# Moving the maxima's transposes, the gates' matmuls and ScalarE's layer norms inside one round of the attention

## The chip, the core and the metric

The program runs on one core of a Trainium2 chip. The metric is the device time of one execution in microseconds (us). The engines are TensorE (PE in the views; PEld is its weight load), VectorE (DVE), ScalarE (ACT), GpSimd (POOL) and SyncE (SP), which here only issues DMAs. Each runs its own list of instructions in order, and they meet at semaphores.

## What is computed

A decoder block on `x` of 16 sequences of 256 tokens of width 256. The change touches the first of its three parts, and the layer norm and gates of the second:

```python
x = x + attn(layernorm(x), W_qkv, W_out)                  # causal, 16 heads of 16
x = x + xattn(layernorm(x), ctx, ctx, ifgate_w, ifgate_b, outnorm_w)
x = x + ffn(layernorm(x), router_w, router_b, up, down)   # 8 experts, top 2

# in attn
attn = softmax(q @ k.T * scale + causal_mask)
out = (attn @ v).reshape(B, -1, S); y = einsum('bds,nhd->bsd', out, W_out)
# in xattn, an mLSTM in its parallel form: gates from concat(q, k, v) @ ifgate_w.T + ifgate_b
```

## The kernel before, in words

The kernel has three stages, one after the other: the attention with the preparation of the second part (`attn_steps`, to about 365 us), the mLSTM (`mlstm_steps`), and the experts. The change is in the first alone.

`attn_steps` yields the steps of 22 rounds `i` from -2 to 21. All five engines walk the same list in the same order, and each does its own part of a step. So a step that is moved in the list moves on every engine that has work in it, and on no other. In a full round, for sequence `b = i`:

- `S1` (two, P = 0 and 1) and `S0`: bf16 scores (L505 a mask, L513 the products), from which VectorE takes row maxima (L897, L902) into `mxn`. `Mp` splits the maxima into two bf16 parts (L910, L912), TensorE transposes them (L639), and ScalarE copies them to `MT` (L1227).
- `T0` (two) and `T2`: transposed scores in f32 (L532) with the maxima added (L537), for sequence `i-1`. ScalarE takes exponentials (L1179 behind `T0`, L1185 behind `T2`), two of 128x1024 for each step, GpSimd zeroes above the diagonal (L1338). `PV`: attention times values for `i-2` (L554), copied to `OTs` (L1191). `A4`: transposes of it for `i-2` (L599), scaled by VectorE (L921 to L925) and sent through DRAM by DMA.
- `QK` and `VX`: projections of sequences `i+1` and `i` (L568, L581); the second half of `VX` transposes what came back for `i-3` (L590), which VectorE adds to `x` (L916).
- Layer norms: `A0s` and `A6s` are the statistics (VectorE L840 to L845, GpSimd L1311 and L1314). `A0n` and `A6n` are ScalarE's two instructions that apply them: `xn` for `i+2`, and `QN` for `i-4` (both L1158). `AX` has TensorE transpose `QN` and then `xn` (L614). ScalarE and VectorE split each into two bf16 parts (L1218 and L933 for `QN`, L1223 and L938 for `xn`). `A6c` does the same with the context (L1210, L1350).
- `MG` is the last step of a round: the gates of sequence `i-5` (L630, 24 matmuls of 16 columns; VectorE adds the bias to `Gq`, L943), then the transposes of the maxima of `i`, in the same pair of banks.

PSUM is used as four pairs of banks. The steps that need one (a user) take them in turn, and user n waits until user n-4 has been read:

```python
def pair_of(*user):
    return pairs[place[user] % 4]
def pair_free(w, *user):
    i = place[user]
    ...
    kind, b, *u = users[i - 4]
```

So a user that is added or moved also changes who waits for whom. A full round has 19 users before and after the change. In the rounds that have no gates yet (`i` below 5), it has 19 before and 18 after. Before, the end of a round is, in order, `VX`, `A6n`, `T2`, `Mp` (VectorE's part), `A4`, `AX`, `MG`, and the next round begins with `S1`, `T0`, `PV`.

Of the kernel before, what the change touches and what calls it, by code (L numbers as in the profile page):

```python
# [71 lines left out]
def attn_steps():  # L72


    for i in range(-2, B + 6):
        if ok(i):
            yield "load", 2 * i, 0
            yield "load", 2 * i + 1, 0
            yield "S1", i, 0
        if ok(i - 1):  # L80
            yield "T0", i - 1, 0
        if ok(i - 2):
            yield "PV", i - 2, 0
        if ok(i + 2):
            yield "A0s", i + 2, 0
        if ok(i):
            yield "S1", i, 1
            yield "split", 2 * i, 0
        if ok(i + 1):
            yield "QK", i + 1, 0  # L90
        if ok(i - 4):
            yield "A6s", i - 4, 0
        if ok(i + 2):
            yield "A0n", i + 2, 0
        if i == -2:
            yield "weights", 0, 0
        if ok(i - 1):
            yield "T0", i - 1, 1
        if ok(i):
            yield "S0", i, 0  # L100
            yield "split", 2 * i + 1, 0
        if i > B and ok(i - 2):
            yield "A4", i - 2, 0
        if ok(i) or ok(i - 3):
            yield "VX", i, 0
        if ok(i - 4):
            yield "A6n", i - 4, 0
        if ok(i - 1):
            yield "T2", i - 1, 0
        if ok(i):  # L110
            yield "Mp", i, 0
        if ok(i - 4):
            yield "A6c", i - 4, 0
        if i <= B and ok(i - 2):
            yield "A4", i - 2, 0
        if ok(i + 2) or ok(i - 4):
            yield "AX", i, 0
        if ok(i) or ok(i - 5):
            yield "MG", i, 0
# [59 lines left out]
def build(nc, x, ctx_in, ctx_t, wqkv, wout, wg, bg, gain, wr, br, wup, wdn, cst, out):  # L179
# [6 lines left out]
    with st:  # L186
# [176 lines left out]
        for kind, b, P in steps:  # L363
            if kind in ("S1", "T0"):
                users += [(kind, b, P, u) for u in range(2)]
            elif kind in ("S0", "T2"):
                users += [(kind, b, u) for u in range(2)]
            elif kind in ("QK", "VX", "PV", "A4", "AX", "MG") or (kind, b) == ("weights", 2):
                users.append((kind, b))
# [5 lines left out]
        def pair_free(w, *user):  # L375
# [21 lines left out]
            elif kind == "A4":  # L397
                w.wait_ge(on_.sem, on_.at(b))
            elif kind == "AX":
                w.wait_ge(xl_.sem, xl_.at(b + 2))  # L400
                w.wait_ge(qnl.sem, qnl.at(b - 4))
            elif kind == "MG":
                w.wait_ge(mt_.sem, mt_.at(b))
                w.wait_ge(ga_.sem, ga_.at(b - 5))
# [80 lines left out]
        def tensor_attn(e, w):  # L485
            for kind, b, P in steps:
# [129 lines left out]
                elif kind == "MG":  # L616
                    pair_free(w, "MG", b)
                    ps = pair_of("MG", b)
                    if ok(b - 5):
                        m = b - 5  # L620
                        v = spl(m)
                        w.wait_ge(cl_.sem, cl_.at(m))
                        w.wait_ge(qnl.sem, qnl.at(m))
                        w.wait_ge(wgs, 1)
                        for tt in range(2):
                            n = 0
                            for sx in range(2):
                                for dk in range(2):
                                    for hx, hw in ((0, 0), (0, 1), (1, 0)):
                                        t = e.matmul(ps[:, 1, 16 * tt:16 * tt + 16], v[:, sx, hx, dk, 128 * tt:128 * tt + 128],  # L630
                                                     WGs[:, dk, hw, 16 * sx:16 * sx + 16], start=n == 0, stop=n == 11, skip_group_check=True)
                                        n += 1
                        t.then_inc(gate.sem, 1)
                    if ok(b):
                        bb = ps[:, 0, :].bitcast(BF)
                        w.wait_ge(mp_.sem, mp_.at(b))
                        for a in range(2):
                            for tt in range(2):
                                t = e.transpose(bb[:, 256 * a + 128 * tt:256 * a + 128 * tt + 128],  # L639
                                                Mp[:, tt, a, :, :].rearrange("p n c -> p (n c)"), idb[:, :])  # L640
                        t.then_inc(mpT.sem, 1)
# [242 lines left out]
        def vector_attn(e, w):  # L884
            for kind, b, P in steps:
# [19 lines left out]
                elif kind == "Mp":  # L905
# [255 lines left out]
        def scalar_attn(e, w):  # L1161
            for kind, b, P in steps:
# [481 lines left out]
```

## Time and profile before

| what | us |
|---|---|
| median of 3 runs (1127.26 to 1127.62) | 1127.43 |
| the profiled execution, its time | 1128.98 |
| its span in the trace | 1127.2 |
| busy: PE 885.7, DVE 691.3, POOL 576.1, ACT 473.0 | |

In the timelines a row is a run of like instructions: start, duration from the first start to the last end, engine, line and operation, tiles written and read, and in brackets how long the engine had been idle and what released it. Neighbours on one engine overlap by some 0.1 us, since an instruction's end is counted until its results have landed; so the distance between two starts is what a step takes of its engine.

### The profile page before, as it was taken

What the parts mean: (1) busy time and instruction counts of PE and PEld (TensorE: products, weight loads), DVE (VectorE), ACT (ScalarE), POOL (GpSimd) and SP (SyncE); (2) the same over time, 40 slices, a digit from 0 to 9 for tenths busy, and PEclk for the clock granted to TensorE, in tenths of its full rate; (3) what the DMA queues carried; (4) which work ended last, traced back from release to release, by engine and by line L of the source; (5) the groups of instructions that cost most, each with busy time, mean ns of one, the idle gap of its engine ahead of it and who ended that gap; (6) DMA issues with size and microseconds to landing.
All of it is one profiled execution on the core that took longest, in us unless ns stands there. A gap on an engine that the chain in (4) does not pass through costs nothing.

```text
span 1127.2 us, 31616 instructions
## 1 busy us (share of the span) xinstructions
PE 885.7 (79%) x11680; PEld 670.1 (59%) x11768; DVE 691.3 (61%) x1524; ACT 473.0 (42%) x842; POOL 576.1 (51%) x784
## 2 busy tenths in 40 slices
PE   5888999998982187677666640699999999999995
PEld 3566666665652065455444520578787787787874
DVE  4767776766652667787877873355555555555553
ACT  2656666665652153443443421233333333333331
POOL 2455565646552455677777775134434434344433
PEclk8999999998986598988999965799999999999998
DMA  8113334342335232333333323233333333333322
GB/s 260 39 40 70 110 77 123 74 123 69 90 96 149 78 114 69 114 112 104 115 118 108 103 88 113 72 49 50 49 50 49 50 49 50 49 49 51 48 40 24
DMA packets 130350, 92.48 MB, mean 82 GB/s; under 512 B 74176, under 2 KB 111168, under 8 KB 130080
## 3 DMA queue, kind: packets, MB, share of 16 engines
q1 hardware_dynamic: 116784, 72.10, 23.4%
q0 software_dynamic: 13296, 17.83, 9.5%
q8 instruction: 104, 1.70, 0.6%
q10 hardware_dynamic: 128, 0.53, 0.2%
q14 instruction: 38, 0.31, 0.1%
HBM read 54.38 MB, written 37.12 MB: 81 GB/s over the span
## 4 chain that ended last, share of the span: by engine, by line
PE 52%; DVE 13%; POOL 11%; ACT 9%; DMA 6%; issue 6%; SPq 1%; POOLq 1%; DVEq 0%; ACTq 0%
PE pair L807 17%; PE pair L820 9%; PE pair L822 7%; POOL sm L1387 4%; PE pair L568 4%; PE pair L554 3%; PE pair L532 3%; DVE SD L1006 2%; DMA o_scr<-On 2%; POOL SD L1379 2%; PE pair L581 2%; DMA STG<-wup_in 2%; POOL xs_scr L1395 1%; PE pair L778 1%; DVE hh L1040 1%
## 5 line engine op out<-in xcount | busy, mean ns | idle before, releaser
L807 PE MATMUL pair<-XTs,WU 128*128 128x128 bf16 x3408 | 285.4, 220 | 5.2 <-issue 2.7
L807 PEld LDWEIGHTS pair<-XTs,WU 128*128 x3408 | 239.2, 98 | 72.9 <-issue 8.6
L1420 POOL DMA_INDIRECT out_d<-XB x71 | 114.0, 1606 | 241.1 <-DVE XB L1150 223.2
L820 PE MATMUL pair<-WD,Hh 128*128 x480 | 181.5, 379 | 0.0
L1294 ACT ACTIVATE Hf<-pair 128x512 f32<-128x512 f32 x142 | 84.8, 597 | 224.4 <-PE pair L807 224.4
L1141 DVE CAST Hh<-Hf 128x512 bf16<-128x512 f32 x142 | 62.9, 443 | 177.1 <-ACT Hf L1294 177.1
L822 PE MATMUL pair<-WD,Hl 128*128 x568 | 154.9, 273 | 4.7
L1338 POOL TENSOR_SCALAR_AFFINE_SELECT PT<-PT 128x512 f32<-128x512 f32 (+1 forms) x96 | 74.4, 788 | 71.3 <-ACT PT L1179 62.8
L707 PE MATMUL pair<-QB,QC 128*128 128x256 bf16 (+1 forms) x768 | 87.2, 253 | 22.0 <-DVE SD L1006 21.2
L1143 DVE TENSOR_TENSOR Hl<-Hf,Hh 128x512 bf16<-128x512 f32 x142 | 99.8, 703 | 4.9
L1249 ACT ACTIVATE SD<-pair 128x512 f32<-128x512 f32 (+1 forms) x128 | 60.9, 492 | 98.4 <-PE pair L699 96.1
L1379 POOL TENSOR_SCALAR_AFFINE_SELECT SD<-SD 128x256 f32<-128x256 f32 x128 | 57.7, 457 | 76.5 <-DVE SD L1006 75.7
L897 DVE TENSOR_REDUCE mxn<-pair 128x4 f32<-128x1024 f32 x64 | 75.2, 1217 | 27.8 <-PE pair L513 27.7
L1006 DVE TENSOR_TENSOR SD<-pair,SD 128x512 f32<-128x512 f32 (+1 forms) x128 | 70.6, 553 | 28.9 <-ACT SD L1249 19.1
L707 PEld LDWEIGHTS pair<-QB,QC 128*128 128x128 bf16 x768 | 61.3, 100 | 36.4 <-DVE SD L1006 21.7
L1179 ACT ACTIVATE PT<-pair 128x1024 f32<-128x1024 f32 x64 | 62.0, 1025 | 37.0 <-PE pair L537 37.0
L1395 POOL DMA_INDIRECT xs_scr<-XB,WGf x64 | 68.2, 1066 | 18.1 <-issue 16.5
L532 PE MATMUL pair<-Q,K 32*128 32x128 f32 (+1 forms) x1024 | 66.4, 360 | 13.1 <-DVE Gq L943 7.7
L1408 POOL TENSOR_SCALAR ix<-XB,TE 128x1 f32<-128x1 f32 x71 | 64.8, 912 | 17.9 <-DMA XB<-xs_scr 17.9
L532 PEld LDWEIGHTS pair<-Q,K 32*128 32x128 f32 x1024 | 42.3, 189 | 26.6 <-ACT MT L1227 14.3
L902 DVE TENSOR_REDUCE mxn<-pair 128x8 f32<-128x1024 f32 x32 | 37.7, 1220 | 33.0 <-PE pair L513 33.0
L699 PE MATMUL pair<-WD 128*128 128x256 bf16 (+1 forms) x256 | 43.9, 254 | 17.7 <-DMA WD<-g_scr 11.5
(217 smaller groups left out, 1824.5 us busy)
## 6 DMA issues: line engine op xcount, KB each, us to landing
XB<-xs_scr SPq DMA_DIRECT2D x71, 130.0 KB, 2.1
STG<-wup_in SPq DMA_DIRECT2D x32, 256.0 KB, 4.4
q_scr<-SPL SPq DMA_DIRECT2D x16, 512.0 KB, 4.0
STG<-wdn_in SPq DMA_DIRECT2D x32, 256.0 KB, 2.8
o_scr<-On SPq DMA_DIRECT2D x32, 128.0 KB, 4.1
Mm<-o_scr SPq DMA_DIRECT2D x16, 256.0 KB, 2.9
CnT<-ctxt_in SPq DMA_DIRECT2D x16, 256.0 KB, 4.1
QC<-q_scr SPq DMA_DIRECT2D x16, 256.0 KB, 3.3
```

Of the source, the lines that this page charges most:

```text
L532: e.matmul(o, K[rows, r, par, a, k0:k0 + 128], Q[rows, r, a, 256 - wd:256], start=True, stop=False, skip_group_check=True)
L707: t = e.matmul(sbk[:, wd * dk:wd * dk + wd], v[:, hc, dk, s0:s0 + 128], q[:, hq, dk, t0:256], start=n == 0, stop=n == 2)
L807: t = e.matmul(upb[r][k][:, 128 * (fm % 4):128 * (fm % 4) + 128], WU[:, bass.ds(reg[j] * 4096 + off, 128)], XTs[:, r, hx, dk, :], start=n ...
L820: e.matmul(yb[r][:, 0:512], Hh[:, r, hsl], WD[:, bass.ds(reg[i] * 4096 + 512 * fk, 512)], start=fk == 0, stop=False, skip_group_check=True)
L822: t = e.matmul(yb[r][:, 0:256], Hl[:, r, hsl], WD[:, bass.ds(reg[i] * 4096 + 512 * fk, 256)], start=False, stop=fk == 7, skip_group_check= ...
L897: e.tensor_reduce(mxn[:, 1, P, 2 * u:2 * u + 2, :], pair_of("S1", b, P, u)[:, :, :].rearrange("p j (r c) -> p j r c", r=2), AX.X, ALU.max, ...
L1006: e.tensor_tensor(SD[:, un % 6, 0:2 * wd], sbb[un % 2][:, 0:2 * wd], SD[:, un % 6, 0:2 * wd], ALU.mult).then_inc(sd_.sem, 1)
L1143: e.tensor_tensor(Hl[:, r, hs], Hf[:, r, hs], Hh[:, r, hs], ALU.subtract).then_inc(hlo.sem, 1)
L1294: e.activation(Hf[:, r, hs], upb[r][k][:, :], ACT.Gelu).then_inc(gel.sem, 1)
L1379: e.affine_select(out=dg, in_=dg, pattern=[[0, 2], [1, 128]], compare_op=ALU.is_ge, fill=0.0, base=0, channel_multiplier=-1).then_inc(sz_. ...
L1395: e.indirect_dma_start(out=xs, out_offset=bass.IndirectOffsetOnAxis(ap=SLI[:, m % 2, k, tt:tt + 1], axis=0), in_=XB[:, 4 * m + tt, :], in_ ...
L1420: e.indirect_dma_start(out=out, out_offset=bass.IndirectOffsetOnAxis(ap=XS[:, i % NX, 256:257].bitcast(I32), axis=0), in_=Yf[:, i % NY, :] ...
```

## The change

`MG` is split into two users. `Mp` now has all of the maxima: VectorE's split of them has become a step of its own, `Mq`, directly behind `S0`. TensorE's transposes stand directly behind `T2`, in a pair of their own, and ScalarE's copy to `MT` behind the exponentials of `T2`. `GA` has the gates, at the round's end, in another pair. `A0n` (`xn`) moves behind the second `T0`, `A6n` (`QN`) behind `T2` and `Mp`.

```diff
         if ok(i - 4):
             yield "A6s", i - 4, 0
+        if ok(i - 1):
+            yield "T0", i - 1, 1
         if ok(i + 2):
             yield "A0n", i + 2, 0
         if i == -2:
             yield "weights", 0, 0
-        if ok(i - 1):
-            yield "T0", i - 1, 1
         if ok(i):
             yield "S0", i, 0
+            yield "Mq", i, 0
             yield "split", 2 * i + 1, 0
         if i > B and ok(i - 2):
             yield "A4", i - 2, 0
         if ok(i) or ok(i - 3):
             yield "VX", i, 0
-        if ok(i - 4):
-            yield "A6n", i - 4, 0
         if ok(i - 1):
             yield "T2", i - 1, 0
         if ok(i):
             yield "Mp", i, 0
         if ok(i - 4):
+            yield "A6n", i - 4, 0
             yield "A6c", i - 4, 0
         if i <= B and ok(i - 2):
             yield "A4", i - 2, 0
         if ok(i + 2) or ok(i - 4):
             yield "AX", i, 0
-        if ok(i) or ok(i - 5):
-            yield "MG", i, 0
+        if ok(i - 5):
+            yield "GA", i - 5, 0
...
-            elif kind in ("QK", "VX", "PV", "A4", "AX", "MG") or (kind, b) == ("weights", 2):
+            elif kind in ("QK", "VX", "PV", "A4", "AX", "Mp", "GA") or (kind, b) == ("weights", 2):
                 users.append((kind, b))
...
-            elif kind == "MG":
+            elif kind == "Mp":
                 w.wait_ge(mt_.sem, mt_.at(b))
-                w.wait_ge(ga_.sem, ga_.at(b - 5))
+            elif kind == "GA":
+                w.wait_ge(ga_.sem, ga_.at(b))
```

The rest of the diff cuts the bodies of the five engines along the same line: what stood under `MG` stands under `GA` or `Mp`, and VectorE's `Mp` under `Mq`. No instruction is added or left out, and the lists of GpSimd and SyncE are the same.

ScalarE over a good half of a round, before, from the second copy of the keys to `MT` (`t0m`, `t2m`: scores are there; `rstd`: GpSimd's part of the statistics; `qT`, `xT`, `mpT`: the transposes of `QN`, `xn`, `Mp`):

```order
L1199 ACTIVATE K<-pair,CF 128x512
L1158 ACTIVATE xn<-XB,LS 128x256 [waits rstd]
L1158 ACTIVATE xn<-XB,LS 128x256
L1179 ACTIVATE PT<-pair 128x1024 [waits t0m] x2
L1204 ACTIVATE Vp<-pair 128x2x16x16 [waits vmm]
L1158 ACTIVATE QN<-XB,LS 128x256 [waits rstd]
L1158 ACTIVATE QN<-XB,LS 128x256
L1185 ACTIVATE PT<-pair 128x1024 [waits t2m] x2
L1210 ACTIVATE SPL<-CnT 128x512 [waits gate,l_sp0,l_cx]
L1218 ACTIVATE SPL<-pair 128x512 [waits qT]
L1223 ACTIVATE xTh<-pair 128x512 [waits xT]
L1227 ACTIVATE MT<-pair 128x512 [waits mpT]
```

And with the change:

```order
L1199 ACTIVATE K<-pair,CF 128x512
L1179 ACTIVATE PT<-pair 128x1024 [waits t0m] x2
L1158 ACTIVATE xn<-XB,LS 128x256 [waits rstd]
L1158 ACTIVATE xn<-XB,LS 128x256
L1204 ACTIVATE Vp<-pair 128x2x16x16 [waits vmm]
L1185 ACTIVATE PT<-pair 128x1024 [waits t2m] x2
L1227 ACTIVATE MT<-pair 128x512 [waits mpT]
L1158 ACTIVATE QN<-XB,LS 128x256 [waits rstd]
L1158 ACTIVATE QN<-XB,LS 128x256
L1210 ACTIVATE SPL<-CnT 128x512 [waits gate,l_sp0,l_cx]
L1218 ACTIVATE SPL<-pair 128x512 [waits qT]
L1223 ACTIVATE xTh<-pair 128x512 [waits xT]
```

`xn` has gone behind the exponentials of the second `T0` (L1179), `QN` behind those of `T2` (L1185) and behind `MT`, which itself has come up from the round's last place.

TensorE at the end of a round and the beginning of the next, before; only the first instruction of each step, with its waits (`qn_`, `xn_`: `QN`, `xn` are written; `ex0`, `ex2`: exponentials done; `mx0`, `mx1`: maxima taken; `x1_`, `v_`: both halves of `VX` read; `on_`: `A4` read):

```order
L599 MATMUL pair3<-CF,OTs 128x4x32 [waits mx0]
L614 MATMUL pair0<-CF,QN 128x128 [waits qn_,x1_,v_]
L614 MATMUL pair0<-CF,xn 128x128 [waits xn_]
L630 MATMUL pair1<-WGs,SPL 128x16 [waits wgs,cl_,ex2]
L639 MATMUL pair1<-idb,Mp 128x128 [waits mp_]
L505 MATMUL pair2<-mkb,idb 128x2x128 [waits ex2]
L505 MATMUL pair3<-mkb,idb 128x2x128 [waits on_]
```

And with the change, where the same lines have one number more, to the first `T0`:

```order
L639 MATMUL pair0<-idb,Mp 128x128 [waits mp_,mx0]
L600 MATMUL pair1<-CF,OTs 128x4x32 [waits x1_,v_]
L615 MATMUL pair2<-CF,QN 128x128 [waits qn_,ex2]
L615 MATMUL pair2<-CF,xn 128x128 [waits xn_]
L629 MATMUL pair3<-WGs,SPL 128x16 [waits cl_,ex2]
L506 MATMUL pair0<-mkb,idb 128x2x128 [waits mt_]
L506 MATMUL pair1<-mkb,idb 128x2x128 [waits on_]
L533 MATMUL pair2<-Q,K 128x256 [waits ga_,qnl,xl_]
```

The transposes of the maxima (L639) have gone ahead of those of `OTs`, which now wait for `x1_`; the transposes of `QN` still wait for `qn_`, and stand at the same distance behind `T2` but for the four instructions of L639. The first `T0` waits for `ga_`, VectorE's sum of the gates.

## Rows read from the trace of the kernel before

**Rows 1.** TensorE's waits, 40 to 300 us: total us, times, longest.

```profile
PE pair L581 <- ACT PT L1179: 12.2, 13, 0.9
PE pair L532 <- DVE Gq L943: 7.0, 9, 1.0
```

**Rows 2.** Timeline of TensorE: start us, us, engine, line, operation [idle before <-releaser].

```profile
215.72 0.28 PE L581 MATMUL pair<-WQh,xTh 128*128 128x256 bf16 x1 [0.94 <-ACT PT L1179]
...
219.06 1.09 PE L599 MATMUL pair<-CF,OTs 128*128 128x128 f32 x8
219.99 0.60 PE L614 MATMUL pair<-CF,QN 128*128 128x128 f32 x4
...
220.86 0.75 PE L630 MATMUL pair<-WGs,SPL 128*128 128x16 bf16 x24
221.46 0.38 PE L639 MATMUL pair<-idb,Mp 128*128 128x128 bf16 x4
221.68 0.88 PE L505 MATMUL pair<-mkb,idb 128*128 128x256 bf16 x4
...
223.66 0.71 PE L532 MATMUL pair<-Q,K 32*128 32x256 f32 x8 [0.76 <-DVE Gq L943]
...
243.05 0.71 PE L532 MATMUL pair<-Q,K 32*128 32x256 f32 x8 [0.76 <-DVE Gq L943]
```

**Rows 3.** Timeline of ScalarE, same stretch.

```profile
219.15 1.94 ACT L1185 ACTIVATE PT<-pair 128x1024 f32<-128x1024 f32 x2 [0.34 <-PE pair L537]
...
220.98 0.63 ACT L1210 ACTIVATE SPL<-CnT 128x512 bf16<-128x512 f32 x1
...
221.97 0.61 ACT L1223 ACTIVATE xTh<-pair 128x512 bf16<-128x512 f32 x1
222.45 0.62 ACT L1227 ACTIVATE MT<-pair 128x512 bf16<-128x512 bf16 x1
...
233.04 1.09 ACT L1158 ACTIVATE xn<-XB,LS 128x256 f32<-128x256 f32 x2
234.03 1.94 ACT L1179 ACTIVATE PT<-pair 128x1024 f32<-128x1024 f32 x2
```

**Rows 4.** Timeline of VectorE, same stretch.

```profile
217.68 0.69 DVE L916 TENSOR_TENSOR XB<-pair,XB 128x512 f32<-128x512 f32 x1 [0.50 <-PE pair L590]
...
223.34 0.18 DVE L943 TENSOR_TENSOR Gq<-pair,BG 128x32 f32<-128x32 f32 x1
```

**Rows 5.** VectorE on the maxima's tile Mp: ns min/median/max.

```profile
L910 DVE CAST Mp<-mxn x10: 194/631/1133, 102.1 to 281.3; 128x32 bf16<-128x32 f32 x10
L912 DVE TENSOR_TENSOR Mp<-mxn,Mp x10: 231/554/1248, 102.3 to 282.2; 128x32 bf16<-128x32 f32 x10
```

**Rows 6.** Timeline of TensorE, the one round with a late QN.

```profile
261.18 0.63 PE L614 MATMUL pair<-CF,QN 128*128 128x128 f32 x4 [2.26 <-ACT QN L1158]
```

**Rows 7.** Timeline of ScalarE in that round.

```profile
259.95 1.09 ACT L1158 ACTIVATE QN<-XB,LS 128x256 f32<-128x256 f32 x2 [3.33 <-POOL LS L1314]
```

**Rows 8.** Stretches: us, busy us (instructions) of PE, PEld, DVE, ACT, POOL, granted clock, DMA.

```profile
254.49:265.42 10.93, 7.93 (x120) 6.29 (x121) 6.43 (x12) 6.35 (x10) 8.40 (x12) 0.87 0.25 30
265.42:278.74 13.32, 12.37 (x169) 7.66 (x169) 7.54 (x15) 6.66 (x10) 6.03 (x11) 0.85 0.39 119
262.75:269.25 6.50, 5.76 (x64) 3.33 (x64) 4.73 (x10) 3.37 (x7) 3.55 (x5) 0.50 0.67 141
320.75:327.25 6.50, 5.65 (x64) 3.38 (x68) 2.17 (x7) 2.74 (x4) 4.29 (x6) 0.50 0.65 146
```

**Rows 9.** Stretch with a wait of 1.40 us: us, PE busy, clock, DMA.

```profile
334.50:337.50 3.00, 1.60 (x41) 1.00 0.26 28
```

**Rows 10.** Timeline of TensorE at the end of the attention's full rounds.

```profile
318.39 0.63 PE L614 MATMUL pair<-CF,QN 128*128 128x128 f32 x4 [1.16 <-ACT QN L1158]
...
321.60 1.24 PE L532 MATMUL pair<-Q,K 32*128 32x256 f32 x8 [1.40 <-ACT MT L1227]
...
335.98 2.81 PE L554 MATMUL pair<-PT,Vp 128*32 128x256 f32 x64 [1.40 <-POOL PT L1338]
```

More of the change, by code:

```diff
@@ L615, in tensor_attn @@
                         t.then_inc((qT if x_ else xT).sem, 1)
[L616 to L624, printed above, removed]
-                        for tt in range(2):
[L626 to L641, printed above, removed]
@@ new lines, in tensor_attn @@
+                elif kind == "GA":
+                    pair_free(w, "GA", b)
+                    ps = pair_of("GA", b)
+                    v = spl(b)
+                    w.wait_ge(cl_.sem, cl_.at(b))
+                    w.wait_ge(qnl.sem, qnl.at(b))
+                    w.wait_ge(wgs, 1)
+                    for tt in range(2):
+                        n = 0
+                        for sx in range(2):
+                            for dk in range(2):
+                                for hx, hw in ((0, 0), (0, 1), (1, 0)):
+                                    t = e.matmul(ps[:, 1, 16 * tt:16 * tt + 16], v[:, sx, hx, dk, 128 * tt:128 * tt + 128],
+                                                 WGs[:, dk, hw, 16 * sx:16 * sx + 16], start=n == 0, stop=n == 11, skip_group_check=True)
+                                    n += 1
+                    t.then_inc(gate.sem, 1)
+                elif kind == "Mp":
+                    pair_free(w, "Mp", b)
+                    bb = pair_of("Mp", b)[:, 0, :].bitcast(BF)
+                    w.wait_ge(mp_.sem, mp_.at(b))
+                    for a in range(2):
+                        for tt in range(2):
+                            t = e.transpose(bb[:, 256 * a + 128 * tt:256 * a + 128 * tt + 128],
+                                            Mp[:, tt, a, :, :].rearrange("p n c -> p (n c)"), idb[:, :])
+                    t.then_inc(mpT.sem, 1)
@@ L904, in vector_attn @@
                                         AX.X, ALU.max, negate=True).then_inc(mx0.sem, 1)
-                elif kind == "Mp":
+                elif kind == "Mq":
                     w.wait_ge(mx1.sem, mx1.at(b, 1, 1))
@@ L939, in vector_attn @@
                                         ALU.subtract).then_inc(xl_.sem, 1)
-                elif kind == "MG" and ok(b - 5):
-                    m = b - 5
+                elif kind == "GA":
+                    m = b
                     w.wait_ge(gate.sem, gate.at(m))
-                    e.tensor_tensor(G[:, 2 * m:2 * m + 2, :], pair_of("MG", b)[:, 1, 0:32].rearrange("p (t c) -> p t c", c=16),
+                    e.tensor_tensor(G[:, 2 * m:2 * m + 2, :], pair_of("GA", b)[:, 1, 0:32].rearrange("p (t c) -> p t c", c=16),
                                     BG[:, 0:16].rearrange("p (a c) -> p a c", a=1).broadcast_to([128, 2, 16]), ALU.add).then_inc(ga_.sem, 1)
@@ L1223, in scalar_attn @@
                         e.activation(xTh[:, m % 2, :, :], ps[:, 0, :].rearrange("p (k c) -> p k c", k=2), ACT.Copy).then_inc(xh_.sem, 1)
-                elif kind == "MG" and ok(b):
+                elif kind == "Mp":
                     w.wait_ge(mpT.sem, mpT.at(b))
                     w.wait_ge(t2m.sem, t2m.at(b - 1, 1))
-                    e.activation(MT[:, :, :], pair_of("MG", b)[:, 0, 0:256].bitcast(BF).rearrange("p (a c) -> p a c", a=2), ACT.Copy).then_inc(mt_.sem, 1)
+                    e.activation(MT[:, :, :], pair_of("Mp", b)[:, 0, 0:256].bitcast(BF).rearrange("p (a c) -> p a c", a=2), ACT.Copy).then_inc(mt_.sem, 1)
             e.drain().then_inc(end_a, 1)
```

## Prediction

> **What bounds the kernel now.** I read the waits of TensorE first, since it is busy for 885.7 of 1127.2 us and for nine tenths of the attention's rounds; then one round's timeline on each engine that it waits for; then the places where the granted clock falls.
>
> Between 40 and 300 us TensorE waits in two places of each round: 13 times 0.94 us before `VX`, for the first exponentials of the second `T0`, and 9 times some 0.77 us before the first `T0`, for the gates' sum `Gq` [rows 1]. In the round of [rows 2] these are the brackets at 215.72 and 223.66; everything else follows back to back. The round takes 243.05 - 223.66 = 19.39 us. From here on I count from the start of `VX`: `T2` ends at 3.34 (the start of L599), `AX` begins at 4.27, the gates' matmuls at 5.14, the maxima's transposes at 5.74, `S1` at 5.96, the first `T0` at 7.94.
>
> The wait of 0.94 has its cause on ScalarE: `xn` begins at 233.04, and the exponentials that `VX` waits for only at 234.03 [rows 3].
>
> **The change part by part.**
>
> *`xn` behind the second `T0`.* The exponentials start 0.99 us sooner, so `VX` starts 0.94 us sooner, where the scores of `S0` end. `xn` itself is wanted at `AX`, 5 us later, and is covered. Gain 0.94 in each of the rounds 1 to 13.
>
> *The maxima behind `S0` and behind `T2`.* VectorE ends `S0`'s maxima 2.5 us or so after the scores, so about when `VX` ends on TensorE. The split of the maxima costs from 0.19 + 0.23 to 1.13 + 1.25 us [rows 5], and the addition to `x`, now behind it, 0.69 [rows 4]. `A4` takes the bank pair of `VX` and so waits for that addition: between 0 and some 2 us. I take 0, because the next wait covers it (below): `A4` needs 0.93 and has to be over by 6.97.
>
> *The gates in a pair of their own.* The first `T0` no longer waits for `MT` in the same breath, but still for `Gq`. Nothing is gained by the split as such.
>
> *`QN` behind the exponentials of `T2`.* This is the term that decides. ScalarE's order is now `T2`'s exponentials, `MT`, `QN`, and TensorE wants `QN` right behind `A4`. `T2`'s scores are whole only at its end, so nothing of this starts earlier. From [rows 3]: the exponentials start at 219.15, that is at 3.43, and the next instruction starts 1.83 later (220.98), at 5.26: `MT`. One of its size holds ScalarE for 0.48 (222.45 - 221.97), so `QN` starts at 5.74 and ends 1.09 later [rows 7] at 6.83; TensorE took it up 0.14 after its end (261.18 against 259.95 + 1.09) [rows 6, 7], so at 6.97. Without the wait it would be there at 3.34 + 0.22 (maxima) + 0.93 (`A4`) = 4.49. A new wait of **2.48 us in each round from 4 to 15**.
>
> From there to the first `T0`: on TensorE `AX` 0.87, gates 0.60, `S1` 1.22 (221.68 to 223.66 less 0.76), so 9.66. Through ScalarE and VectorE: `xTh` can start when `xn`'s transposes have landed, about 1.07 after `AX` starts (estimate: 0.87 and the overlap of some 0.2), and from `xTh` to the first `T0` it is 223.66 - 221.97 = 1.69: 9.73. I take 9.7, against 7.94: 1.76 later, less the 0.94 that `VX` gave. **+0.8 us a round.** Between the first `T0` and the next `VX` nothing else changes.
>
> By rounds, with the clock as it is:
> - 1 to 3 (no `QN` yet): 3 x -0.94 = -2.8
> - 4 to 11 and 13: 9 x 0.8 = +7.2
> - 12: here the statistics of `QN` came late from GpSimd [rows 7], and `AX` waited 2.26 us already [rows 6]. Behind `T2`'s exponentials most of that delay is hidden: `QN` starts some 0.6 later than in the others, so the first `T0` comes at 10.3 after `VX` where it came at 10.93 (`VX` began at 254.49, the `T0` at 265.42) [rows 8]: -0.6, and -0.9 before `VX`. The clock had also fallen (next part), and from the first `T0` to `VX` the round took 13.32 us [rows 8] where 19.39 - 7.94 = 11.45 is normal: -1.9. Together -3.4
> - 14: no `xn`, so nothing to gain before `VX`: +1.7. 15: `QN` comes 1.4 later than at 318.39, but `MT` now comes before it, and `MT` is what the `T0` at 321.60 waited 1.40 us for [rows 10]: +0.3. In the rounds after these the exponentials of `T2` go ahead of `QN` and feed the `PV` at 335.98, which waits for GpSimd behind them [rows 10]; a gain under 1 us that the later `AX` in front of it takes back: 0
>
> Sum: -2.8 + 7.2 - 3.4 + 2.0 = **+3.0 us**.
>
> *The clock.* Behind the 2.26 us wait of round 12 the granted clock was 0.50, the 1.2 GHz level of the two, through all of 262.75 to 269.25 us; it was 0.50 again in 320.75 to 327.25, where waits of 1.16, some 0.2 and 1.40 us stood around 1.5 us of transposes and narrow matmuls [rows 8, 10]. Through a single wait of 1.40 us it stayed at 1.00 [rows 9]. What the fall in round 12 cost: from `AX` to the first `T0` 4.24 us against 3.67 in [rows 2], and the 1.9 us above: 2.4 us. The new wait, 2.48 us (2.0 or more if `A4` comes late), stands in the same place, between `A4` and `AX`, and is nearly as long as the one that was followed by a fall; but one case doesn't say how often. The ends are 0 and 11 falls more (round 15 has one already). The row it is nearest to speaks for more than half: I take 6, so 6 x 2.4 = **+14.4 us**.
>
> Total +17.4 on 1128.98, so 1146.4 for a profiled execution, which stands 1.5 over the median: 1127.4 + 17.4 = 1144.8.
>
> The Trainium skill, in "TensorE: Matmul & The Clock Gate", section "HAM oscillation — how this bites in real kernels", tells of a loop in which the clock falls and recovers in every iteration because each has a long wait in it; its remedy is to keep the matmuls together. It speaks against this change, which gathers two waits under 1 us into one of 2.5. Taken as a rule for every round it makes the sum +3.0 + 11 x 2.4 = 29.4; that is the second rival.
>
> **The rivals.**
>
> *The clock holds.* The wait is there, but no fall follows it, as none followed 1.40. For it: round 12 is a single case, and its wait was a single piece, while a late `A4` would break this one in two. Time: 1127.4 + 3.0 = 1130.4, and the uncertainty of the walk, some 2.5 us in 12 rounds of which each step was read once, gives 1128 to 1133. Chance 0.18.
>
> *The clock falls in every round with the wait.* For it: the nearest row. Against it: the wait may come in two pieces, and only two falls could be read. Time: 1127.4 + 29.4 = 1156.8. Chance 0.17.
>
> *The maxima come late.* If VectorE needs the 2.4 us for the split beside GpSimd [rows 5], and the addition is followed by `A4` so late that it ends behind 6.97, each such round loses what is over, up to 0.5 us: 12 x 0.5 = 6, on top of the forecast: 1151. Chance 0.06.
>
> *Faster: `QN` is no brake.* ScalarE, between `T2`'s end and `AX`, at 4.49, would need `QN` in 1.15 us where I read 3.5. It decides from the point at which `QN` ends before 5.5: then the first `T0` comes at 5.5 + 2.7 = 8.2, under the 7.94 + 0.94 that breaks even with what `VX` gains. Were it so in all rounds, both waits of [rows 1] go: 13 x 0.94 + 9 x 0.77, and the 4.9 us of round 12: 24 us, so 1103. Against it: the order of ScalarE's instructions is fixed, and the two exponentials alone end at 5.4. Chance 0.08, which also stands for a walk that is wrong by its sign with the clock holding (1122 to 1126).
>
> *The change doesn't do what it says.* It means to take the maxima off the round's end. If they are not ready behind `T2`, TensorE only waits for them there instead; up to 2.4 us of such a wait lies inside the wait for `QN` and costs nothing, so this is part of the forecast and has no chance of its own.
>
> **How the numbers follow.** Forecast (the wait, and the clock falls in some rounds, 2 to 9 of 11): 0.51, 1136 to 1152, at 1145. With the clock holding 0.18, always falling 0.17, late maxima 0.06, faster 0.08. The range from 1129 to 1157 leaves out the faster case, half of the edges of the two clock cases, and so about 2 in 10. A measurement of this kernel can tell 0.2%, 2.3 us: below 1125.2 is faster, 0.08; between 1125.2 and 1129.7 is the lower part of the clock-holds case, 0.07; the rest is slower, 0.85.
>
> **What would show it.** Right: in rounds 4 to 15 the wait before L581 is gone; TensorE waits some 2.5 us before the transposes of `QN` for ScalarE; the wait for `Gq` is under 0.3; the exponentials of the second `T0` follow the copies of the keys at once; stretches with a clock of 0.50 behind some of the new waits. Wrong: no wait for `QN`, or one under 1 us; a clock of 1.00 from 40 to 300 us (then 1130); waits of TensorE for `x1_` or the maxima before L599 or L639 that reach beyond `QN`.

## The result, and the profile after

The changed kernel takes 1138.36 us (median of 4 runs, 1137.78 to 1139.53) against 1127.35: a ratio of 1.0103, 95% interval 1.0085 to 1.0120 (the ratios here are of the mean times, so they differ a little from those of the medians). Its profiled execution took 1138.52 us with a span of 1136.8. It is slower by 11 us, where 17.4 had been forecast.

The waits of TensorE from 40 to 300 us (total, times, longest), which answer to [rows 1]:

```profile
PE pair L615 <- ACT QN L1158: 15.5, 10, 2.2
PE pair L639 <- DVE Mp L912: 6.4, 10, 1.1
PE pair L533 <- DVE xTl L938: 4.0, 3, 1.5
PE pair L533 <- DVE Gq L943: 2.7, 7, 0.4
PE pair L600 <- DVE XB L916: 1.6, 9, 0.2
```

The 13 waits for the exponentials before `VX` are gone. In their place stand waits for `QN`, for the maxima, and short ones for the addition to `x`; and in the rounds that have no `QN` yet, three waits for `xTl`, VectorE's low part of `xn`, of up to 1.5 us. Between `VX` and `VX` in the middle of the attention this is TensorE's timeline, as [rows 2]:

```profile
222.26 0.28 PE L582 MATMUL pair<-WQh,xTh 128*128 128x256 bf16 x1
...
226.53 0.38 PE L639 MATMUL pair<-idb,Mp 128*128 128x128 bf16 x4 [0.86 <-DVE Mp L912]
227.09 1.07 PE L600 MATMUL pair<-CF,OTs 128*128 128x128 f32 x8 [0.18 <-DVE XB L916]
229.24 0.63 PE L615 MATMUL pair<-CF,QN 128*128 128x128 f32 x4 [1.08 <-ACT QN L1158]
...
232.06 0.71 PE L533 MATMUL pair<-Q,K 32*128 32x256 f32 x8 [0.39 <-DVE Gq L943]
...
252.34 0.71 PE L533 MATMUL pair<-Q,K 32*128 32x256 f32 x8 [0.39 <-DVE Gq L943]
```

From the start of `VX` (L582) the first `T0` (L533) comes at 9.80 us, where it came at 7.94; the round is 252.34 - 232.06 = 20.28 us, where it was 19.39. Between `T2`'s end and `QN`'s transposes TensorE stands still three times, 0.86, 0.18 and 1.08 us. ScalarE in the same round, as [rows 3]:

```profile
221.18 1.95 ACT L1179 ACTIVATE PT<-pair 128x1024 f32<-128x1024 f32 x2
222.98 1.11 ACT L1158 ACTIVATE xn<-XB,LS 128x256 f32<-128x256 f32 x2
...
225.70 1.94 ACT L1185 ACTIVATE PT<-pair 128x1024 f32<-128x1024 f32 x2 [1.11 <-PE pair L538]
227.52 0.60 ACT L1227 ACTIVATE MT<-pair 128x512 bf16<-128x512 bf16 x1
228.00 1.09 ACT L1158 ACTIVATE QN<-XB,LS 128x256 f32<-128x256 f32 x2
```

The exponentials of `T0` (221.18) go ahead of `xn`, and those of `T2` (225.70), `MT` and `QN` follow each other until 229.09, 0.15 us before L615 starts. 229.24 is 6.98 after `VX`. In none of the rounds 4 to 13 does `QN` wait here for GpSimd's part of the statistics; in the kernel before it does in two, for 3.7 us in all.

The clock, as [rows 8]: between 60 and 300 us it fell behind the waits for `QN` of rounds 4, 9 and 13, each time for some 3.5 us, as here:

```profile
209.25:212.75 3.50, 3.50 (x51) 2.41 (x51) 2.96 (x5) 0.56 (x2) 1.70 (x2) 0.52 0.50 55
```

To say where the time went I set the start of each `PV` (L554, L555) beside that of the kernel before:

| round | PV starts, before | changed | later by |
|---|---|---|---|
| 2 | 52.52 | 53.06 | 0.54 |
| 4 | 89.37 | 89.94 | 0.57 |
| 5 | 108.61 | 110.83 | 2.22 |
| 9 | 186.16 | 191.91 | 5.75 |
| 10 | 205.57 | 213.09 | 7.52 |
| 12 | 244.35 | 253.64 | 9.29 |
| 13 | 267.87 | 273.91 | 6.04 |
| 14 | 287.98 | 295.05 | 7.07 |
| 17 | 335.98 | 344.06 | 8.08 |

The gates' stage that follows the attention starts at 379.7 instead of 372.9: 6.8 us. The other 2.9 us of the span lie in the mLSTM stage, 345.6 us here and 342.7 before, whose instructions are the same. In the twelve traces of this study that stage takes from 342.2 to 345.6 us; whether the attention's order has a part in that isn't shown. So for each run I give two numbers: the ratio of the times, and the start of the gates' stage in its trace, which is the attention alone, but of one execution. That of the kernel before was one of its slower ones (1128.98 us against medians of 1124.9 to 1127.4), so, as an estimate, a start measured against its 372.9 can flatter a kernel by up to some 2 to 4 us; kernels are best compared with each other by it, and with before by the ratio.

### The profile page after: what moved, and what is told of

Same layout as the page of the kernel before. It is cut to its first block, busy times and chain, and to the rows that moved or that the text cites. A ratio compares the mean times of both kernels' runs of the same rounds, so it can differ in the third digit from the quotient of the medians.

```text
span 1136.8 us, 31719 instructions
## 1 busy us (share of the span) xinstructions
PE 896.8 (79%) x11768; PEld 675.5 (59%) x11768; DVE 686.2 (60%) x1524; ACT 473.8 (42%) x842; POOL 579.3 (51%) x784
## 4 chain that ended last, share of the span: by engine, by line
PE 55%; DVE 11%; POOL 10%; ACT 6%; issue 6%; DMA 2%; POOLq 1%; SPq 1%; another core or an unknown queue 0%; DVEq 0%; ACTq 0%
PE pair L807 17%; PE pair L820 11%; PE pair L822 5%; PE pair L533 4%; POOL sm L1387 4%; PE pair L555 3%; PE pair L569 3%; DVE SD L1006 2%; PE pair L506 2%; POOL xs_scr L1395 2%; ACT PT L1185 2%; PE pair L582 2%; POOL SD L1379 2%; DVE hh L1040 1%; PE pair L778 1%
## 5 line engine op out<-in xcount | busy, mean ns | idle before, releaser
L820 PE MATMUL pair<-WD,Hh 128*128 x568 | 214.8, 379 | 0.0
L707 PE MATMUL pair<-QB,QC 128*128 128x256 bf16 (+1 forms) x768 | 90.4, 259 | 19.9 <-DVE SD L1006 18.9
L1179 ACT ACTIVATE PT<-pair 128x1024 f32<-128x1024 f32 x64 | 62.1, 1029 | 47.9 <-PE pair L538 47.9
L1395 POOL DMA_INDIRECT xs_scr<-XB,WGf x64 | 68.1, 1064 | 18.1 <-issue 16.2
L533 PE MATMUL pair<-Q,K 32*128 32x128 f32 (+1 forms) x1024 | 68.7, 369 | 10.6 <-DVE xTl L938 4.0
L533 PEld LDWEIGHTS pair<-Q,K 32*128 32x128 f32 x1024 | 43.8, 195 | 24.4 <-issue 13.1
L699 PE MATMUL pair<-WD 128*128 128x256 bf16 (+1 forms) x256 | 44.9, 259 | 16.2 <-DMA WD<-g_scr 11.1
L820 PEld LDWEIGHTS pair<-WD,Hh 128*128 128x128 bf16 x568 | 55.5, 98 | 1.9 <-issue 0.4
## 6 DMA issues: line engine op xcount, KB each, us to landing
o_scr<-On SPq DMA_DIRECT2D x32, 128.0 KB, 4.1
```

What stands on the lines that cost most here:

```text
L533: e.matmul(o, K[rows, r, par, a, k0:k0 + 128], Q[rows, r, a, 256 - wd:256], start=True, stop=False, skip_group_check=True)
L707: t = e.matmul(sbk[:, wd * dk:wd * dk + wd], v[:, hc, dk, s0:s0 + 128], q[:, hq, dk, t0:256], start=n == 0, stop=n == 2)
L820: e.matmul(yb[r][:, 0:512], Hh[:, r, hsl], WD[:, bass.ds(reg[i] * 4096 + 512 * fk, 512)], start=fk == 0, stop=False, skip_group_check=True)
L1395: e.indirect_dma_start(out=xs, out_offset=bass.IndirectOffsetOnAxis(ap=SLI[:, m % 2, k, tt:tt + 1], axis=0), in_=XB[:, 4 * m + tt, :], in_ ...
```

## The experiments

| kernel | ratio to before (95%) | gates' stage starts at |
|---|---|---|
| before | 1 | 372.9 |
| changed | 1.0103 (1.0085 to 1.0120) | 379.7 |
| e1_qn_back | 1.0026 (1.0008 to 1.0044) | 371.1 |
| e2_xn_only | 0.9930 (0.9904 to 0.9956) | 363.9 |
| e3_qn_only | 1.0161 (1.0136 to 1.0186) | 387.5 |
| e4_split_only | 1.0133 (1.0107 to 1.0158) | 383.5 |
| e5_split_context_last | 1.0062 (1.0038 to 1.0087) | 376.2 |
| e6_change_mended | 1.0000 (0.9983 to 1.0017) | 365.8 |
| e7_xn_context_last | 0.9890 (0.9862 to 0.9919) | 356.8 |
| e8_gates_in_wait | 1.0135 (1.0109 to 1.0161) | 384.9 |
| e9_maxima_late_early_rounds | 1.0088 (1.0064 to 1.0111) | 373.6 |
| e10_change_again | 1.0107 (1.0088 to 1.0126) | 381.0 |

### The parts apart: e1 to e4

**e1_qn_back**: the changed kernel, `QN` as before.

```diff
+        if ok(i - 4):
+            yield "A6n", i - 4, 0
         if ok(i - 1):
             yield "T2", i - 1, 0
...
         if ok(i - 4):
-            yield "A6n", i - 4, 0
             yield "A6c", i - 4, 0
```

> The changed kernel with only QN's step put back ahead of T2. Theory Q (the order of QN behind T2's exponentials is the whole cost): the wait of TensorE before QN's transposes is gone in rounds 4 to 15 except round 12, and what is left is the 0.94 us gained before VX: 13 x 0.94 under before, about 1115 us. Rival M (the maxima behind T2 cost as much, hidden under the wait for QN): TensorE still waits up to 1 us for the maxima and 0.18 for the addition to x before A4, VectorE's chain from A4 to the gates' sum starts later by that, and a round takes from VX to the first T0 about 9.0 us (9.80 in the changed kernel, 7.94 + 0.94 before): about 1128 us.

Measured: 1.0026, and a round as long as the rival had it. The waits from 40 to 300 us, and the first `T0` 9.13 us after `VX`:

```profile
PE pair L534 <- DVE Gq L944: 9.9, 9, 1.4
PE pair L640 <- DVE Mp L913: 3.8, 7, 0.8
```

```profile
195.00 0.28 PE L583 MATMUL pair<-WQh,xTh 128*128 128x256 bf16 x1
...
204.13 0.71 PE L534 MATMUL pair<-Q,K 32*128 32x256 f32 x8 [1.44 <-DVE Gq L944]
```

The wait for `QN` is gone and most of the loss with it; but the 12 us that `xn` should have gained are not there. So the order of `QN` is not the whole cost. The rival's number came out, but not by its mechanism: on ScalarE `QN` waits in this round 0.84 us for GpSimd's part of the statistics, which puts `T2`'s exponentials 0.73 us later behind `VX` than before, and `MT` behind them takes another 0.48 (see e4). Together that is the 1.2 us from 7.94 to 9.13. In rounds 7 and 8, where `QN` doesn't wait, the first `T0` comes at 8.43.

**e2_xn_only**: the kernel before, `xn` behind the second `T0`.

```diff
+        if ok(i - 1):
+            yield "T0", i - 1, 1
         if ok(i + 2):
             yield "A0n", i + 2, 0
         if i == -2:
             yield "weights", 0, 0
-        if ok(i - 1):
-            yield "T0", i - 1, 1
```

> The kernel before with one part of the change alone: xn's step behind the second T0. Both theories: VX no longer waits for the first exponentials, VX to first T0 stays at 7.9 us, 13 rounds x 0.94 = 12 us under before, 1115 us. Rival G (the gain is given back at the next wait, as in rounds 1 to 3 of the changed kernel, since the exponentials that VX waited for stood on a chain that VectorE sets): VX to first T0 grows by 0.5 to 0.9 us, 1122 to 1127 us.

Measured: 0.9930, the gates' stage 9.0 us sooner of the 12.2. That lies between the two expectations. The wait before `VX` is gone; in some rounds `VX` to `T0` stays at 7.95 us, in others most of the gain is lost again before the first `T0`, as in this one (8.82 us):

```profile
134.23 0.28 PE L581 MATMUL pair<-WQh,xTh 128*128 128x256 bf16 x1
...
143.05 0.71 PE L532 MATMUL pair<-Q,K 32*128 32x256 f32 x8 [1.57 <-DVE Gq L943]
```

```profile
137.56 1.09 ACT L1158 ACTIVATE QN<-XB,LS 128x256 f32<-128x256 f32 x2 [1.00 <-POOL LS L1314]
138.56 1.91 ACT L1185 ACTIVATE PT<-pair 128x1024 f32<-128x1024 f32 x2
```

The cause stands on ScalarE. `VX` comes sooner, but in this round GpSimd's part of the statistics doesn't keep up, so `QN`, which stands ahead of `T2`'s exponentials here, waits for it, and they start 4.33 us after `VX` instead of 3.43. `QN` waits so in six of the rounds 4 to 13, for 5.8 us in all. That also says what the late place of `QN` in the changed kernel is good for: it hides this wait, and pays for it in every round.

This part alone is the one that gains.

**e3_qn_only**: the kernel before, `QN` behind `T2`.

```diff
-        if ok(i - 4):
-            yield "A6n", i - 4, 0
         if ok(i - 1):
             yield "T2", i - 1, 0
...
         if ok(i - 4):
+            yield "A6n", i - 4, 0
             yield "A6c", i - 4, 0
```

> The kernel before with one part alone: QN's step behind T2. Theory Q: TensorE waits 2.2 us before QN's transposes in rounds 4 to 15, VX to first T0 goes from 7.94 to about 9.4 us, 12 x 1.5 less the 4 us of round 12 whose late QN it hides: 1139 to 1143 us, with or without falls of the clock. Theory M alone: no more than 3 us over before.

Measured: 1.0161, or 1141.7 us, and `VX` to `T0` 9.32 us: as expected. (The kernel before took 1124.9 us beside it, so the loss, 17 to 18 us, is somewhat more than the walk's; the clock fell three times between 60 and 300 us here.) The waits are in ten rounds the ones that the walk had, 2.1 us each:

```profile
PE pair L613 <- ACT QN L1157: 20.6, 10, 2.1
```

**e4_split_only**: the changed kernel, both layer norms as before; only the maxima and the gates have moved.

```diff
-        if ok(i - 1):
-            yield "T0", i - 1, 1
         if ok(i + 2):
             yield "A0n", i + 2, 0
...
+        if ok(i - 1):
+            yield "T0", i - 1, 1
...
+        if ok(i - 4):
+            yield "A6n", i - 4, 0
         if ok(i - 1):
             yield "T2", i - 1, 0
...
-            yield "A6n", i - 4, 0
             yield "A6c", i - 4, 0
```

> The changed kernel with both layer norms at their old places, so that only the maxima and the gates have moved. Theory Q: nothing, 1126 to 1128 us. Rival M: the exponentials before VX still cost 0.94, which gives VectorE time for the maxima, so the wait behind T2 is under 0.5 us and the round changes by -0.3 to +0.5: 1123 to 1134 us; a wait of TensorE for Mp in 12 rounds with a sum over 3 us would speak for M.

Measured: 1.0133, well outside both: the split alone costs 10.6 us in the attention. TensorE's waits for the maxima sum to only 2.0 us, so the rival doesn't explain it either. ScalarE's timeline shows what neither had:

```profile
229.96 1.94 ACT L1186 ACTIVATE PT<-pair 128x1024 f32<-128x1024 f32 x2 [0.34 <-PE pair L539]
231.78 0.60 ACT L1228 ACTIVATE MT<-pair 128x512 bf16<-128x512 bf16 x1
232.26 0.64 ACT L1211 ACTIVATE SPL<-CnT 128x512 bf16<-128x512 f32 x1
232.78 0.61 ACT L1219 ACTIVATE SPL<-pair 128x512 bf16<-128x512 f32 x1
233.25 0.62 ACT L1224 ACTIVATE xTh<-pair 128x512 bf16<-128x512 f32 x1
```

```profile
226.52 0.28 PE L583 MATMUL pair<-WQh,xTh 128*128 128x256 bf16 x1 [0.94 <-ACT PT L1180]
...
234.95 0.71 PE L534 MATMUL pair<-Q,K 32*128 32x256 f32 x8 [1.25 <-DVE Gq L944]
```

```profile
233.42 0.69 DVE L934 TENSOR_TENSOR SPL<-pair,SPL 128x512 bf16<-128x512 f32 x1 [0.50 <-ACT SPL L1219]
```

`MT` (L1228) now stands between `T2`'s exponentials and the copies of `QN` and `xn` (L1219, L1224). `xTh` starts 3.29 us behind the exponentials, where it was 221.97 - 219.15 = 2.82 in [rows 3], and what hangs on it, VectorE's `xTl` and `Gq` and then the first `T0`, comes at 8.43 us after `VX` instead of 7.94: VectorE stands still for 0.50 us until the copy of `QN` (L1219) is there, and from then to `Gq` it works back to back. The scores that use `MT` don't need it sooner than before. The prediction has these 0.48 us of `MT` in its walk to `QN`, but it put the price of the split as such at nothing.

This chain isn't all of the 10.6 us. It is 0.49 in each of nine rounds, 4.4 us. Rounds 1 to 3 lose 2.5 (57.04 us from the `VX` of round 1 to that of round 4, against 54.58 before), for which e9 has the cause. And the clock fell three times, each time at the first `T0` or just behind it, so that `T0` and `PV` ran at the 1.2 GHz level; that costs 1.6 us each (a round of 21.47 beside ones of 19.87), where the kernel before has one fall, in round 12. The rest is differences of both signs in single rounds.

### The chain on ScalarE: e5 to e7

If that is the cause, any other copy taken out of the chain gives the time back. The context's copy (`A6c`, L1210 before) stands in it too, and isn't wanted until the next round. In each of these three kernels this is the edit, made to e4, e1 and e2:

```diff
         if ok(i - 4):
-            yield "A6c", i - 4, 0
...
+        if ok(i - 4):
+            yield "A6c", i - 4, 0
         if i == -1:
             yield "weights", 1, 0
```

> The kernel with the split alone, and the context's copy and its low part (A6c, L1210 and L1350) moved from before AX to the end of the round. Theory C (what the split costs is that MT's copy, 0.48 us, now stands on ScalarE between T2's exponentials and the copies of QN and xn, a chain that ends in the first T0): taking another 0.52 us copy out of that chain gives the time back, VX to first T0 from 8.4 back to 7.9 us, 6 us or more under e4: ratio to before at most 1.008. Rival M (waits of TensorE for the maxima are the cost): no change from e4, ratio 1.013.

Measured: 1.0062, 7.3 us sooner than e4 at the gates' stage, and `VX` to `T0` 7.92 us:

```profile
224.91 1.94 ACT L1186 ACTIVATE PT<-pair 128x1024 f32<-128x1024 f32 x2 [0.34 <-PE pair L539]
226.73 0.60 ACT L1228 ACTIVATE MT<-pair 128x512 bf16<-128x512 bf16 x1
227.21 0.62 ACT L1219 ACTIVATE SPL<-pair 128x512 bf16<-128x512 f32 x1
227.69 0.63 ACT L1224 ACTIVATE xTh<-pair 128x512 bf16<-128x512 f32 x1
228.16 0.66 ACT L1211 ACTIVATE SPL<-CnT 128x512 bf16<-128x512 f32 x1
```

```profile
221.47 0.28 PE L583 MATMUL pair<-WQh,xTh 128*128 128x256 bf16 x1 [0.94 <-ACT PT L1180]
...
229.39 0.71 PE L534 MATMUL pair<-Q,K 32*128 32x256 f32 x8 [0.74 <-DVE Gq L944]
```

```profile
227.86 0.69 DVE L934 TENSOR_TENSOR SPL<-pair,SPL 128x512 bf16<-128x512 f32 x1
```

`xTh` starts 2.78 us behind the exponentials, and VectorE no longer waits before L934. The step also moves GpSimd's part of the copy (L1350), but the instructions of VectorE from L926 on take as long in both traces, so the 0.5 us a round are ScalarE's. They are not all of the 7.3: e4's three falls of the clock between 60 and 300 us, 4.8 us by the reading above, are not in this trace either, and whether the order keeps them away isn't shown. In the middle rounds nothing of the split's cost is left: the `PV` of rounds 6 to 12 stand 5.9 us behind the kernel before (133.86 against 128.0 to 250.29 against 244.35), neither more nor less. Those 5.9 us are lost up to round 6: 2.3 before the `VX` of round 1, 2.5 in rounds 1 to 3 (below) and 0.8 in round 5, whose `QN` waits 1.15 us for GpSimd. Round 12, where the kernel before had its late `QN`, gives 3.4 back.

> The changed kernel with QN back ahead of T2 and the context's copy at the end of the round. Theory C: 0.5 us a round under e1, whose ratio was 1.0026: 0.997. Rival: no change from e1, because VectorE's chain (A4, then QN's and xn's low parts) ends last there.

Measured: 1.0000, by the trace 5.3 us sooner than e1, which is what was expected, but by the ratios only 0.3% (3 us), half of it. The changed kernel with two of its steps mended is level with the kernel before, no more.

> The kernel before with xn behind the second T0 and the context's copy at the end of the round. Theory C: under e2 (ratio 0.993) by up to 0.5 us a round: 0.988 to 0.990. Rival V (VectorE's own work behind A4, back to back from 220.2 to 223.5 us before, ends at the same time): as e2, 0.993.

Measured: 0.9890, 1113.97 against 1125.93 us, and by the traces 7.1 us sooner than e2. That overstates it: e2's profiled execution was 4 us slower than its median, and it has a fall of the clock in round 9 that this one lacks. By the ratios the step gives 0.4%, and the intervals of the two (0.9862 to 0.9919, 0.9904 to 0.9956) overlap a little. In this round `VX` to `T0` is 8.04 us, without a wait before `VX`:

```profile
206.78 0.28 PE L581 MATMUL pair<-WQh,xTh 128*128 128x256 bf16 x1
...
214.82 0.71 PE L532 MATMUL pair<-Q,K 32*128 32x256 f32 x8 [0.65 <-DVE Gq L943]
```

This is a version that beats both kernels: `xn` behind the second `T0`, the context's copy at the round's end, and nothing else. `QN` still waits for GpSimd in six rounds here, 7.5 us in all, so more may be had there; no run tries it.

### The clock, and the rounds without QN: e8 to e10

**e8_gates_in_wait**: the changed kernel, the gates ahead of `A4`.

```diff
+        if ok(i - 5):
+            yield "GA", i - 5, 0
         if i <= B and ok(i - 2):
             yield "A4", i - 2, 0
...
-        if ok(i - 5):
-            yield "GA", i - 5, 0
```

> The changed kernel with the gates' step ahead of A4, so that 0.6 us of matmuls stand inside the wait for QN. By the walk of the prediction: the wait before QN's transposes shrinks by 0.6 where it is one piece, VX to first T0 from 9.8 to 9.4 us, 3 to 5 us under the changed kernel: ratio about 1.006. Theory K (the clock falls where TensorE stands still for about 1.9 us or more in one piece behind A4): no fall of the clock between 60 and 300 us, since the longest wait is some 1.6. Rival: falls as often as in the changed kernel (3 in rounds 4 to 14).

Measured: 1.0135, a miss on both counts. A round without a fall of the clock is 20.13 us instead of 20.28, since the first `T0` now waits up to 0.84 us for `xTl`; and the clock fell in 5 rounds instead of 3, at 0.7 us each in the rounds after the first of them. Behind this stretch it fell, with no wait over 1.16 us in it:

```profile
186.99 0.38 PE L639 MATMUL pair<-idb,Mp 128*128 128x128 bf16 x4 [1.16 <-DVE Mp L912]
187.51 0.75 PE L629 MATMUL pair<-WGs,SPL 128*128 128x16 bf16 x24
188.11 1.07 PE L600 MATMUL pair<-CF,OTs 128*128 128x128 f32 x8
189.40 1.08 PE L615 MATMUL pair<-CF,QN 128*128 128x128 f32 x4 [0.22 <-ACT QN L1158]
```

So a fall needs no long wait in one piece. That theory is dropped.

**e9_maxima_late_early_rounds**: the changed kernel, the maxima behind `AX` in rounds 0 to 3.

```diff
-        if ok(i):
+        if ok(i) and i >= 4:
             yield "Mp", i, 0
...
+        if ok(i) and i < 4:
+            yield "Mp", i, 0
         if ok(i - 5):
             yield "GA", i - 5, 0
```

The reason is the table of `PV` above: rounds 2 and 3 took as long as before, though each lost its 0.94 of waiting. TensorE in round 3, before and then changed:

```profile
80.87 0.28 PE L581 MATMUL pair<-WQh,xTh 128*128 128x256 bf16 x1 [0.94 <-ACT PT L1179]
...
84.21 1.09 PE L599 MATMUL pair<-CF,OTs 128*128 128x128 f32 x8
...
88.01 0.71 PE L532 MATMUL pair<-Q,K 32*128 32x256 f32 x8
```

```profile
80.46 0.28 PE L582 MATMUL pair<-WQh,xTh 128*128 128x256 bf16 x1
...
84.29 0.38 PE L639 MATMUL pair<-idb,Mp 128*128 128x128 bf16 x4 [0.42 <-DVE Mp L912]
84.86 1.06 PE L600 MATMUL pair<-CF,OTs 128*128 128x128 f32 x8 [0.18 <-DVE XB L916]
...
88.64 0.71 PE L533 MATMUL pair<-Q,K 32*128 32x256 f32 x8 [1.51 <-DVE xTl L938]
```

`A4` (L599, L600) starts 3.34 us after `VX` before, and 4.40 changed: 0.42 of waiting for the maxima, 0.22 for their transposes, 0.18 for `x`, and small gaps. The first `T0` follows `A4` by 3.8 us in both, by way of VectorE, which works back to back from `A4` to `xTl`, while `xTh` is there before it is wanted (0.8 us in the changed kernel).

> The changed kernel, but in rounds 0 to 3, which have no QN, the maxima's transposes and MT's copy stand behind AX as before. Theory M (in these rounds the maxima's wait in front of A4 moves VectorE's chain A4 to xTl, which ends 3.8 us later in the first T0, and gives back the 0.94 of VX): rounds 1 to 3 gain what the prediction gave them, so the gates' stage starts 2.5 to 3.5 us sooner than in the changed kernel (379.7 us), at 376.2 to 377.2, and VX to first T0 in round 3 goes from 8.2 to 7.2 us; ratio to before about 1.007. Rival (the loss comes from the pairs' rotation, which has one user fewer in rounds without gates either way): no difference from the changed kernel, 8.2 us.

Measured: the gates' stage at 373.6, 6.1 us sooner. `VX` to `T0` in round 3 is 7.14 us, rounds 2 and 3 take 17.26 and 17.67 us where they took 18.23 and 18.65, and the `PV` of round 2 starts at 50.29 instead of 53.06:

```profile
76.72 0.28 PE L584 MATMUL pair<-WQh,xTh 128*128 128x256 bf16 x1
...
83.86 0.71 PE L535 MATMUL pair<-Q,K 32*128 32x256 f32 x8
```

From the `VX` of round 1 to that of round 4 it takes 51.72 us, as e2 and e7 do, where the changed kernel takes 54.15 and the one before 54.58. So with the maxima behind `AX` these rounds gain 2.86 us, the forecast's 2.8, and the place of the maxima takes 2.4 of them back. The rest of the 6.1 isn't shown to be the edit's: 2.3 us lie before the `VX` of round 1, where traces of one and the same list of steps differ by up to 1.8 (e2 is there at 44.73 us, e7 at 42.97). The ratio, 1.0088, is not clear of the 1.0107 that the changed kernel has beside it.

**e10_change_again**: the changed kernel, unedited.

> The changed kernel once more, beside the one above on the same chip. Both theories: ratio to before 1.010, gates' stage from 379 to 381 us. It tells whether the falls of the clock come in the same rounds: if they hang on the order alone, behind QN's waits of rounds 4, 9 and 13 again; if on when a round stands against something that runs on its own, in others.

Measured: 1.0107, gates' stage at 381.0. The clock fell in three of the rounds 4 to 14 again, but in rounds 4, 8 and 12, not 4, 9 and 13. In round 8 it fell behind a wait in pieces:

```profile
187.41 0.38 PE L639 MATMUL pair<-idb,Mp 128*128 128x128 bf16 x4 [0.84 <-DVE Mp L912]
...
190.14 1.09 PE L615 MATMUL pair<-CF,QN 128*128 128x128 f32 x4 [1.11 <-ACT QN L1158]
```

```profile
190.50:193.00 2.50, 2.50 (x35) 2.31 (x34) 1.04 (x3) 1.21 (x3) 1.16 (x1) 0.50 0.47 49
```

Both executions had 3 falls in 11 rounds, and not in the same ones. So the order alone doesn't say which rounds a fall hits. What does, these runs don't show.

## Why the prediction was right, and where it was off

- **`QN` behind the exponentials: right, in size and place.** `AX` was put at 6.97 us after `VX` and came at 6.98; the first `T0` at 9.7, measured 9.80. The round was to be 0.8 us longer, it is 0.88. e3 shows the wait alone (2.1 us against the 2.2 that its own walk gave). The wait for `Gq` that is left is 0.39, where under 0.3 had been named as a sign.
- **`xn`: right.** No wait before `VX` in any round; e2 shows it alone as a gain of 9.0 us of the 12.2 reckoned.
- **The wait was forecast as one piece of 2.48 us.** It comes in up to three, since VectorE's split of the maxima (0.34 and 1.23 us in this round) is late for the place behind `T2`. Inside the wait for `QN` that costs nothing, as the prediction says.
- **"I take 0, because the next wait covers it (below)": wrong in rounds 1 to 3.** The cover is the wait for `QN`, and these rounds have no `QN`. The term there was -2.8; measured, from the `VX` of round 1 to that of round 4, it is -0.43. e9 takes the cause away and gets the 2.4 us back. This is the step that failed in the sum without the clock. With what lies before round 1 the miss at the `PV` of round 4 is 3.4 us (+0.57); that other 1.0 is within what traces of the same steps differ by there.
- **"Nothing is gained by the split as such": true, but nothing was put down for its loss.** e4 shows 10.6 us when it stands alone, 4.4 of it by `MT` in ScalarE's chain. In the changed kernel the waits for the maxima lie under `QN` in the middle rounds, but `MT` does not: the first `T0` is at 9.80, where e3, without the split, has it at 9.32. In a middle round the three parts nearly add up (-0.94 + 1.38 + 0.49 = 0.93, measured 0.88). Over the whole attention they don't: alone they come to -9.0, +14.6 and +10.6 us at the gates' stage, together to 6.8 and not 16.2, since each trace has its own falls of the clock and late `QN`s, and round 12 has its delay to give back only once.
- **Round 12: near.** Forecast -3.4 with the whole of its fall. Measured are 6.04 - 9.29 = -3.25 up to the `PV` of round 13, and 0.7 more behind that, since the fall of the kernel before reached into this `PV` (its round 13 took 20.11 us and not 19.39): -4.0 together. The 0.6 by which `QN` was to start later there did not come: the first `T0` is at 9.80, not at 10.3. Round 14: +1.7 forecast, 1.86 measured.
- **The clock: the mechanism right, both sizes off.** Six falls of 2.4 us were taken, 14.4 us. Three came, and cost 0.8 to 0.9 each: rounds 4, 9 and 13 took 20.89, 21.18 and 21.14 us with a fall, against some 20.1 (round 4, an estimate: 19.24 before and the 0.88) and 20.27 without; 2.5 us in all. The price came from round 12 before, where the granted clock stayed at the level of 1.2 GHz for nearly 7 us; here the clock came back to 2.4 GHz after some 3.5, before `PV` began. Six was a choice between 0 and 11, with no rule behind it, so that three came is not a confirmation of it.
- **The rival from the Trainium skill.** In the Trainium skill, "TensorE: Matmul & The Clock Gate", section "HAM oscillation — how this bites in real kernels", the loop that loses its clock in every iteration waits for data from DMA each time, and longer than any wait for `QN` here. To take that for every round was the prediction's own step. It would have made eleven falls; the trace has three, so the measurement decides against the rule in that form.
- **The total.** +3.0 and +14.4 were forecast. In the attention's trace it was +4.3 and +2.5. The first looks closer than it was: up to the `PV` of round 15 it was 6.4 against 2.7 forecast, and from there to the gates' stage 2.1 us came back where +0.3 was put; those last rounds were not taken apart. The mLSTM stage is 2.9 us longer in this trace than in that of the kernel before, and 2.1 in that of e10, for which nothing was forecast and no cause is shown. The measured 1138.36 lies about halfway between the forecast of 1144.8 and the rival in which the clock holds, 1130.4. It is in the range because the misses have opposite signs: the clock's term was 12 us too high, and about half of that was made up by the rest of the attention (1.3), the mLSTM stage (2.9) and the 1.6 by which the profiled execution of the kernel before stood over its median. That part is luck.

What stays open: which rounds a fall hits; why it lasts some 3.5 us in most places and nearly 7 in round 12 before and in round 4 of e10 (about 107.8 to 114.7 us); and why the mLSTM stage differs by up to 3.4 us between traces of the same instructions.

## What to carry to other kernels

When engines walk one list in order, moving a step puts it into every engine's chain: price it on each of them, in front of whatever it passes, also where it seems hidden. A cost that is hidden under another wait is hidden only in the rounds that have that wait, and it comes back when the wait is mended (e1: 8.43 us where it was 7.94); so change one part at a time, since here one of three parts was worth 0.7% and the other two more than ate it. A copy that nobody waits for belongs behind the ones on which the next step hangs: that alone gave 0.3 to 0.7% in three different kernels, of which only the largest is well clear of the noise. And an engine that gets its work sooner meets the next supplier sooner: `xn` alone gave 9 us of 12, since GpSimd's statistics did not keep up with it in six of ten rounds.

## What the runs showed that was not expected

- The granted clock fell to the 1.2 GHz level with no wait over 1.16 us in the stretch before it (e8), and stayed up through seven of ten waits of 2.06 us (e3). Neither a single wait nor its length tells it here; and the same program meets it in other rounds from one execution to the next.
- What a fall cost depended on what ran in it. Of some 3.5 us, it cost 0.7 to 0.9 us where it began at `AX` or just behind it (the changed kernel, e8, e10), and 1.6 where it began at the first `T0` or just behind it and slowed `PV` too (e4). Of nearly 7 us it cost about 2.4 (round 12 before; rounds 4 and 5 of e10, 21.28 and 21.67 us, lose as much together).
- The split of the maxima on VectorE, two instructions on 32 columns, takes 0.42 us at its fastest and 1.6 in the round shown; in the traces the long ones stand beside copies and subtractions of GpSimd. No run takes GpSimd's work away, so that this is the cause was not tried.
